# First weights and first rows of two stages loaded in the stage ahead, and a third place for turned chunks

## The chip, the cores and the metric

The kernel runs on one core of a Trainium2 chip. The metric is the device time of one execution in microseconds (us), as a median of several runs. The engines named here are TensorE (PE; PEld is its weight load), VectorE (DVE), ScalarE (ACT), GpSimd (POOL) and SyncE (SP), whose queue (SPq) issues most of the DMAs.

## The reference

A transformer block with conditioning, and behind it a rotation of each row within a 64-dimensional subspace. Four sequences of 1024 rows, 576 columns wide:

```python
ada = silu(c) @ W_ada + b_ada
shift_msa, scale_msa, gate_msa, shift_mlp, scale_mlp, gate_mlp = split(ada, 6)
h = modulate(layernorm(x), shift_msa, scale_msa)
x = x + gate_msa * attention(h, W_qkv, b_qkv, W_proj, b_proj)
h = modulate(layernorm(x), shift_mlp, scale_mlp)
x = x + gate_mlp * (gelu(h @ W_fc1 + b_fc1) @ W_fc2 + b_fc2)   # FF = 2304
U, _ = qr(P)                                                   # 576 x 64
R = expm(A(cond))                                              # 64 x 64 for each sequence
z = x @ U
out = x + (z @ R - z) @ U.T
```

## The kernel before, in words

The kernel is a sequence of stages with a barrier of all engines between them; each stage makes its own tiles and semaphores, and what passes from one to the next goes through DRAM. Products are made in float32 precision from two parts: a high part (rounded to float32r) and a low part (the difference), so that a float32 product is three passes. The last four stages are attention, `stage_proj`, `stage_mlp` and `stage_rotate`. The 4096 rows are taken in groups of 512 (`GT`), eight in all; in the feed-forward in groups of 256 (`GM`), sixteen in all.

**Projection (`stage_proj`).** For each of the eight groups TensorE spreads reciprocal sums, projects the attention's output, and turns the normalised rows into the operand of the feed-forward. ScalarE writes the operand's high parts to `ht`, GpSimd the low parts, and SyncE stores each of the five chunks to `h2_s` (line 1219). GpSimd adds the rows onto `x2_s` by an accumulating DMA (line 1252). SyncE's program is written out in order: loads of later groups, the five stores of this one, the wait for the accumulating DMA. Before its loop it loads the operand of the third group with lines 139 and 142.

**Feed-forward (`stage_mlp`).** All of `w1` (576 x 2304, two parts) and `w2` lie in SBUF, loaded in nine parts (`PARTS`) of two blocks (`PF`) of 128 hidden columns each. SyncE issues, in this order: `bias1` (line 1553), the first half group's operand `ht` (line 1544), then for each part four DMAs of `w1` (lines 65 and 67) and two of `w2` (line 1560), then the second `ht`, the gates and the `x` rows. TensorE runs two blocks ahead with `first` (14 matmuls, line 1655) and follows with `second` (12 matmuls, line 1669); between them ScalarE applies GELU (1593), VectorE makes the high part (1616), GpSimd the low part (1607). `first` waits for part `f // PF` of `w1` where a part begins, `second` for that of `w2`. At the end of a group VectorE adds and SyncE stores to `x3_s` (1571).

**Rotation (`stage_rotate`).** SyncE loads the rows of group 0 (line 1732), two parts of the rotated basis `ro` (1736), the basis `u` (1740), then the rows of group 1, and later those of group g + 2 within group g. GpSimd makes the identity matrix (146, 148) and pads the last 64 columns to 128 (1760). For each group TensorE turns five chunks of 512 x 128 (1817), each into one of two PSUM places, which chunk k takes as k % 2 (`c_slot`); ScalarE copies the high part (1769), VectorE subtracts for the low part (1787), and only then is the place free. Ten matmuls make z (1831), ScalarE and VectorE split it (1776, 1794), TensorE turns the next group's chunks, then makes y with 24 matmuls (1844), and VectorE adds the rows (1802). VectorE takes the next group's five low parts ahead of this group's eight sums; TensorE's 13th y matmul waits for the first sum.

## Time and profile before

| | |
|---|---|
| median of 3 runs | 3061.78 us (3058.14 to 3062.56) |
| the profiled execution | 3062.73 us |
| its span | 3061.1 us |
| TensorE busy | 2805.0 us, 92% |
| VectorE, ScalarE, GpSimd busy | 55%, 46%, 47% |
| feed-forward: SyncE's first issue, TensorE's first matmul | 1982.46, 1994.43 |
| rotation: SyncE's first issue, TensorE's first transpose | 2958.78, 2964.66 |

All times in rows are us from the span's start, durations of a single instruction ns where marked. The slices and the windows say what share of a stretch an engine was busy; the granted clock is TensorE's, as a share of its full 2.4 GHz, and the DMA share is the mean over 16 DMA engines. In a timeline an idle time stands in brackets, with what ended it. A busy TensorE isn't a TensorE at its peak, since the ends of matmuls are modelled.

### The profile page before, as it was taken

What the parts mean: (1) busy time and instruction counts of PE and PEld (TensorE: products, weight loads), DVE (VectorE), ACT (ScalarE), POOL (GpSimd) and SP (SyncE); (2) the same over time, 40 slices, a digit from 0 to 9 for tenths busy, and PEclk for the clock granted to TensorE, in tenths of its full rate; (3) what the DMA queues carried; (4) which work ended last, traced back from release to release, by engine and by line L of the source; (5) the groups of instructions that cost most, each with busy time, mean ns of one, the idle gap of its engine ahead of it and who ended that gap; (6) DMA issues with size and microseconds to landing.
All of it is one profiled execution on the core that took longest, in us unless ns stands there. A gap on an engine that the chain in (4) does not pass through costs nothing. (4 is left out here: it accounts for less than half of the span.)

```text
span 3061.1 us, 51443 instructions
## 1 busy us (share of the span) xinstructions
PE 2805.0 (92%) x16066; PEld 2272.3 (74%) x16066; DVE 1680.9 (55%) x3417; ACT 1416.8 (46%) x1835; POOL 1437.3 (47%) x1073
## 2 busy tenths in 40 slices
PE   7859999969999999999999879689999999999977
PEld 3248878846666666666666568589999999999976
DVE  4446777558999999999999657511111111111126
ACT  2112322229999999999999836511111111111112
POOL 1232333128888888888888836512222222222210
PEclk8769999979999999999999989899999999999989
DMA  5476675653443434343343259892112111211126
GB/s 191 136 245 228 228 249 196 234 170 85 89 93 83 95 81 94 85 90 91 85 96 81 71 165 289 246 310 74 37 38 66 46 38 37 74 38 37 53 74 217
DMA packets 336907, 377.68 MB, mean 123 GB/s; under 512 B 162816, under 2 KB 226952, under 8 KB 336764
## 3 DMA queue, kind: packets, MB, share of 16 engines
q1 hardware_dynamic: 327162, 356.66, 39.0%
q0 software_dynamic: 4224, 9.44, 1.7%
q10 hardware_dynamic: 5382, 9.67, 1.0%
q8 instruction: 95, 1.56, 0.2%
q14 instruction: 44, 0.36, 0.0%
HBM read 225.77 MB, written 158.93 MB: 126 GB/s over the span
## 5 line engine op out<-in xcount | busy, mean ns | idle before, releaser
L896 POOL TENSOR_TENSOR a_pl<-a_pf,a_ph 128x1024 fp32r<-128x1024 f32 x384 | 908.6, 2401 | 24.8 <-ACT a_pf L1006 24.8
L929 DVE TENSOR_REDUCE a_mx<-a_psum_s 128x1 f32<-128x512 f32 x992 | 637.5, 684 | 92.4 <-PE a_psum_s L1035 88.5
L1004 ACT ACTIVATE a_ph<-a_psum_t 128x1024 fp32r<-128x1024 f32 x512 | 525.9, 1027 | 133.6 <-PE a_psum_t L1052 126.5
L1607 POOL TENSOR_TENSOR m_al<-m_af,m_ah 128x256 fp32r<-128x256 f32 x288 | 211.1, 733 | 760.1 <-DVE m_ah L1616 760.1
L1655 PE MATMUL m_psum_h<-m_ht,m_w 128*128 128x256 f32 x4032 | 528.1, 283 | 30.2 <-DMA m_w<-w_s 20.5
L1616 DVE CAST m_ah<-m_af 128x256 fp32r<-128x256 f32 x288 | 85.1, 295 | 830.2 <-ACT m_af L1593 830.2
L1655 PEld LDWEIGHTS m_psum_h<-m_ht,m_w 128*128 128x128 f32 x4032 | 504.3, 189 | 33.7 <-issue 32.9
L1593 ACT ACTIVATE m_af<-m_psum_h,m_bias 128x256 f32<-128x256 f32 x288 | 136.4, 473 | 826.7 <-PE m_psum_h L1655 826.7
L1669 PE MATMUL m_psum_y<-m_w,m_ah 128*128 128x288 f32 x2304 | 506.7, 295 | 1.6 <-DVE m_y L1633 1.5
L1071 PE MATMUL a_psum_o<-a_ph,a_vs 128*100 128x512 f32 x1024 | 420.9, 411 | 22.4 <-POOL a_pl L896 18.9
L1072 PE MATMUL a_psum_o<-a_pl,a_vs 128*100 128x512 f32 x1024 | 405.1, 396 | 0.0
L1006 ACT ACTIVATE a_pf<-a_psum_t 128x1024 f32<-128x1024 f32 x384 | 391.2, 1019 | 0.0
L1669 PEld LDWEIGHTS m_psum_y<-m_w,m_ah 128*128 128x128 f32 x2304 | 388.1, 188 | 3.4 <-DVE m_y L1633 2.8
L1052 PE MATMUL a_psum_t<-a_qs,a_ks 110*128 110x512 f32 x1024 | 337.9, 412 | 37.8 <-DVE a_pl L945 31.3
L1669 PE MATMUL m_psum_y<-m_w,m_al 128*128 128x288 f32 x1152 | 341.3, 296 | 0.0
L1035 PE MATMUL a_psum_s<-a_ks,a_qs 108*128 108x512 f32 x992 | 313.9, 397 | 2.5 <-DVE a_mx L929 2.4
L1071 PEld LDWEIGHTS a_psum_o<-a_ph,a_vs 128*100 128x100 f32 x1024 | 168.7, 165 | 150.1 <-POOL a_pl L896 99.7
L1052 PEld LDWEIGHTS a_psum_t<-a_qs,a_ks 110*128 110x128 f32 x1024 | 184.5, 191 | 122.6 <-DVE a_pl L945 82.9
L663 PE MATMUL q_psum_pqk<-q_ht,q_w 128*128 128x512 f32 x1008 | 257.9, 408 | 13.3 <-DMA q_bv<-in_L_cond_b_qkv_dram 13.3
L1035 PEld LDWEIGHTS a_psum_s<-a_ks,a_qs 108*128 108x128 f32 x992 | 188.3, 190 | 64.9 <-DVE a_mx L929 3.6
L663 PEld LDWEIGHTS q_psum_pqk<-q_ht,q_w 128*128 128x128 f32 x1008 | 188.1, 192 | 55.6 <-issue 13.7
L1669 PEld LDWEIGHTS m_psum_y<-m_w,m_al 128*128 128x128 f32 x1152 | 216.6, 188 | 0.0
(232 smaller groups left out, 3059.5 us busy)
## 6 DMA issues: line engine op xcount, KB each, us to landing
a_qs<-q_s SPq DMA_DIRECT2D x192, 144.0 KB
a_ks<-k_s SPq DMA_DIRECT2D x192, 144.0 KB
w_s<-q_ws SPq DMA_DIRECT2D x64, 324.0 KB, 3.5
h_s<-p_ht SPq DMA_DIRECT2D x40, 512.0 KB, 4.7
m_ht<-h_s SPq DMA_DIRECT2D x16, 1280.0 KB, 8.2
v_s<-q_vo SPq DMA_DIRECT2D x64, 288.0 KB, 2.3
a_vs<-v_s SPq DMA_DIRECT2D x128, 144.0 KB, 4.5
q_s<-q_qko SPq DMA_DIRECT2D x32, 512.0 KB, 2.7
```

Of the source, the lines that this page charges most:

```text
L663: i = pe.matmul(pqk[:, m % 3], w[:, k, m * P:(m + 1) * P], ht[:, half, a, :], start=(n == 0), stop=(n == len(PASSES) - 1))
L896: pool.tensor_tensor(pl[:, s % RING], pf[:, s % RING], raw(ph[:, s % RING]), ALU.subtract).then_inc(lo_pool, 1)
L929: dve.tensor_reduce(mx[:, u % 2, t, h:h + 1], p_s[:, h * 512:(h + 1) * 512], AX.X, ALU.max) \
L1004: act.activation(ph[:, s % RING], p_t[:, s % 2], ACT.Exp, scale=SCALE)
L1006: act.activation(full, p_t[:, s % 2], ACT.Exp, scale=SCALE).then_inc(exp_done, 1)
L1035: pe.matmul(p_s[:, h * 512:(h + 1) * 512], qs[0:SROWS, u, t * P:(t + 1) * P], ks[0:SROWS, u, h * 512:(h + 1) * 512], start=True, stop=True) \
L1052: m = pe.matmul(p_t[:, s % 2, r * GT:(r + 1) * GT], ks[0:MROWS, u, t * P:(t + 1) * P], qs[0:MROWS, u, lh * GT:(lh + 1) * GT], start=True, ...
L1071: pe.matmul(p_o[0:VW, lh], vs[:, u, t], ph[:, s % RING, cols], start=(t == 0), stop=False)
L1072: m = pe.matmul(p_o[0:VW, lh], vs[:, u, t], pl[:, s % RING, cols], start=False, stop=(t == KT - 1))
L1607: pool.tensor_tensor(al[:, f % RING], af[:, f % RING], raw(ah[:, f % RING]), ALU.subtract).then_inc(lo_ready, 1)
L1655: m = pe.matmul(p_h[:, f % RING, 0:GM], w1[:, k, f * P:(f + 1) * P], ht[:, q, a], start=(i == 0), stop=(i == len(PASSES) - 1))
L1669: m = pe.matmul(p_y[:, t, a, 0:HALF], part[:, f % RING, t * P:(t + 1) * P], w2[:, s, f, a * HALF:(a + 1) * HALF], start=(f == 0 and i == 0 ...
```

## The change

Three things. (1) The feed-forward's weights part 0, its bias and the first half group's operand get tiles of their own, made before the projection on the right side of SBUF and kept until the end of the kernel (`mlp_tiles`). The projection loads them: the weights and the bias in seven DMAs ahead of SyncE's loop, the operand behind group `NG - 3`. SyncE waits for them at the end of the stage. The feed-forward starts with part 1. (2) When the last but one feed-forward group is stored, SyncE loads the basis `u`, and, once TensorE has done with part 0, the rows of the rotation's groups 0 and 1 into the homes of these weights. The rotation doesn't load them; the padding goes to a tile of its own, in two copies a group. (3) The rotation's turned chunks have three PSUM places instead of two (`SLOTS`).

```diff
@@ -54,6 +54,10 @@
+MLP_PARTS = 9
+MLP_PF = FF // P // MLP_PARTS
...
@@ -131,6 +135,23 @@
+def mlp_tiles(nc, ctx):
+    sb = lambda n, s, d=F32: ctx.enter_context(nc.sbuf_tensor("f_" + n, s, d, side="right"))
+    return {"w1": sb("w1", [P, W_TILES, MLP_PF * P], F32R),
+            "w2": sb("w2", [P, 2, MLP_PF, C], F32R),
+            "ht": sb("ht", [P, A_TILES, GT // 2], F32R),
+            "bias1": sb("bias1", [P, FF // P])}
+def load_mlp_weights(eng, w1, w2, w1_s, w2_s, i, w1_in, w2_in):
+    cols = slice(i * MLP_PF * P, (i + 1) * MLP_PF * P)
+    load_split_weight(eng, w1, w1_s, cols, w1_in)
+    for s in range(2):
+        eng.dma_start(raw(w2[:, s]), w2_s[s, cols].rearrange("(f p) n -> p f n", p=P)).then_inc(w2_in, 16)
...
@@ -1143,6 +1164,7 @@
+        first_w1, first_w2, first_h = sem("first_w1"), sem("first_w2"), sem("first_h")
...
@@ -1204,6 +1226,10 @@
+                load_mlp_weights(sp, first["w1"], first["w2"], w1_s, w2_s, 0, first_w1, first_w2)
+                sp.dma_start(first["bias1"][:], b1.rearrange("(f p) -> p f", p=P),
+                             allow_slow_non_contiguous=True).then_inc(first_h, 16)
...
@@ -1228,6 +1254,14 @@
+                    if g == NG - 3:
+                        for c in range(NK):
+                            sp.wait_ge(h_out[c], START + 16)
+                        sp.dma_start(raw(first["ht"][:]), h2_s[0:1, :, :, 0:GT // 2]
+                                     .rearrange("a p k n -> (a p) k n")).then_inc(first_h, 16)
+                sp.wait_ge(first_h, 32)
+                sp.wait_ge(first_w1, 64)
+                sp.wait_ge(first_w2, 32)
...
@@ -1498,18 +1532,20 @@
-    PARTS = 9
-    PF = FT // PARTS
+    PARTS, PF = MLP_PARTS, MLP_PF
-        w1 = sb("w1", [P, W_TILES, FF], F32R)
-        w2 = sb("w2", [P, 2, FT, C], F32R)
-        bias1 = sb("bias1", [P, FT])
+        w1 = sb("w1", [P, PARTS - 1, W_TILES, PF * P], F32R)
+        w2 = sb("w2", [P, PARTS - 1, 2, PF, C], F32R)
+        bias1 = first["bias1"]
-        ht = sb("ht", [P, 2, A_TILES, GM], F32R)
+        ht1 = sb("ht1", [P, A_TILES, GM], F32R)
+        ht = (first["ht"], ht1)
+        w1_part = [first["w1"]] + [w1[:, i] for i in range(PARTS - 1)]
+        w2_part = [first["w2"]] + [w2[:, i] for i in range(PARTS - 1)]
...
@@ -1518,7 +1554,7 @@
-        bias_in = sem("bias_in")
+        rows_in, u_in = sem("rows_in"), sem("u_in")
...
@@ -1541,7 +1577,7 @@
-                    sp.dma_start(raw(ht[:, q]), h2_s[bass.ds(j, 1), :, :, q * GM:(q + 1) * GM]
+                    sp.dma_start(raw(ht[q][:]), h2_s[bass.ds(j, 1), :, :, q * GM:(q + 1) * GM]
...
@@ -1550,15 +1586,8 @@
-                sp.dma_start(bias1[:], b1.rearrange("(f p) -> p f", p=P),
-                             allow_slow_non_contiguous=True).then_inc(bias_in, 16)
-                load_h(0, 0)
-                for i in range(PARTS):
-                    cols = slice(i * PF * P, (i + 1) * PF * P)
-                    load_split_weight(sp, w1[:, :, cols], w1_s, cols, w1_in[i])
-                    for s in range(2):
-                        sp.dma_start(raw(w2[:, s, i * PF:(i + 1) * PF]),
-                                     w2_s[s, cols].rearrange("(f p) n -> p f n", p=P)).then_inc(w2_in[i], 16)
+                for i in range(1, PARTS):
+                    load_mlp_weights(sp, w1_part[i], w2_part[i], w1_s, w2_s, i, w1_in[i], w2_in[i])
...
@@ -1575,15 +1604,28 @@
+                    if isinstance(n, int) and n == NG - 2:
+                        sp.dma_start(raw(ru[:]), u_s).then_inc(u_in, 16)
+                        for t in range(NT):
+                            sp.wait_ge(y_out[t], START + 16 * 4)
+                        sp.wait_ge(h_ready, FT * (NG - 1) + PF)
+                        sp.dma_start(raw(first["w1"][:]).rearrange("p k n -> p (k n)").rearrange("p (t c) -> p t c", c=C),
+                                     x3_s[0:GT].rearrange("(t p) c -> p t c", p=P)).then_inc(rows_in, 16)
+                        sp.wait_ge(used, RING + FT * (NG - 1) + PF)
+                        sp.dma_start(raw(first["w2"][:]).rearrange("p s f n -> p (s f n)")
+                                     .rearrange("p (t c) -> p t c", c=C),
+                                     x3_s[GT:2 * GT].rearrange("(t p) c -> p t c", p=P)).then_inc(rows_in, 16)
+                sp.wait_ge(u_in, 16)
+                sp.wait_ge(rows_in, 32)
-                act.wait_ge(bias_in, 16)
...
@@ -1645,21 +1687,24 @@
-                    if f == 0:
+                    if f == 0 and q == 1:
-                    if q == 0 and f % PF == 0:
+                    if f == 0 and q == 0 and not (isinstance(n, int) and n == 0):
+                        pe.wait_ge(ht_in[q], 16 * j)
+                    if q == 0 and f >= PF and f % PF == 0:
-                        m = pe.matmul(p_h[:, f % RING, 0:GM], w1[:, k, f * P:(f + 1) * P], ht[:, q, a],
+                        m = pe.matmul(p_h[:, f % RING, 0:GM], w1_part[f // PF][:, k, f % PF * P:(f % PF + 1) * P], ht[q][:, a],
-                    if q == 0 and f % PF == 0:
+                    if q == 0 and f >= PF and f % PF == 0:
...
@@ -1667,7 +1712,7 @@
-                                              w2[:, s, f, a * HALF:(a + 1) * HALF],
+                                              w2_part[f // PF][:, s, f % PF, a * HALF:(a + 1) * HALF],
...
@@ -1688,29 +1733,35 @@
-def stage_rotate(nc, x3_s, u_s, rot_s, out):
+def stage_rotate(nc, x3_s, rot_s, out, first, u):
+    EARLY = 2
+    SLOTS = 3
+    slot = lambda g, c: (NK * g + c) % SLOTS
-        u = sb("u", [P, NK, 2 * R], F32R)
-        xt = sb("xt", [P, NG, SUB, CPAD])
+        xt = sb("xt", [P, NG - EARLY, SUB, C])
+        pad = sb("pad", [P, NG, SUB, P])
+        rows = [raw(first["w1"][:]).rearrange("p k n -> p (k n)").rearrange("p (t c) -> p t c", c=C),
+                raw(first["w2"][:]).rearrange("p s f n -> p (s f n)").rearrange("p (t c) -> p t c", c=C)] \
+            + [xt[:, g] for g in range(NG - EARLY)]
-        p_t = ps("t", [P, 2, GT])
+        p_t = ps("t", [P, SLOTS, GT])
-        u_in, zeroed, ident_made = sem("u_in"), sem("zeroed"), sem("ident_made")
+        zeroed, ident_made = sem("zeroed"), sem("ident_made")
...
@@ -1729,16 +1780,16 @@
-                    sp.dma_start(xt[:, g, :, 0:C], x3_s[g * GT:(g + 1) * GT].rearrange("(t p) c -> p t c", p=P)) \
-                      .then_inc(x_in[g], 16)
+                    if g >= EARLY:
+                        sp.dma_start(rows[g], x3_s[g * GT:(g + 1) * GT].rearrange("(t p) c -> p t c", p=P)) \
+                          .then_inc(x_in[g], 16)
-                load(0)
-                sp.dma_start(raw(u[:]), u_s).then_inc(u_in, 16)
-                for g in range(1, AHEAD):
+                for g in range(AHEAD):
...
@@ -1755,9 +1806,13 @@
-                    pool.wait_ge(x_in[g], 16)
-                    pool.tensor_copy(xt[:, g, :, C:CPAD], xt[:, g, :, FULL * P:C]).then_inc(padded, 1)
+                    if g >= EARLY:
+                        pool.wait_ge(x_in[g], 16)
+                    for r in range(2):
+                        pool.tensor_copy(pad[:, g, :, r * REM:(r + 1) * REM], rows[g][:, :, FULL * P:C]) \
+                            .then_inc(padded, 1)
...
@@ -1766,7 +1821,7 @@
-                        act.activation(xh[:, half, c], p_t[:, c_slot(half, c)], ACT.Copy).then_inc(hi_ready, 1)
+                        act.activation(xh[:, half, c], p_t[:, slot(g, c)], ACT.Copy).then_inc(hi_ready, 1)
...
@@ -1799,7 +1854,7 @@
-                            dve.tensor_tensor(y[:, t, cols], p_y[:, t % 2, a, 0:HALF], xt[:, g, t, cols],
+                            dve.tensor_tensor(y[:, t, cols], p_y[:, t % 2, a, 0:HALF], rows[g][:, t, cols],
...
@@ -1807,20 +1862,20 @@
-                    pe.wait_ge(x_in[g], 16)
+                    if g >= EARLY:
+                        pe.wait_ge(x_in[g], 16)
-                            pe.wait_ge(padded, g + 1)
-                        if NK * g + c >= 2:
-                            pe.wait_ge(lo_ready, NK * g + c - 1)
+                            pe.wait_ge(padded, 2 * (g + 1))
+                        if NK * g + c >= SLOTS:
+                            pe.wait_ge(lo_ready, NK * g + c - SLOTS + 1)
-                            i = pe.transpose(p_t[:, c_slot(half, c), t * P:(t + 1) * P],
-                                             xt[:, g, t, c * P:(c + 1) * P], ident[:])
+                            i = pe.transpose(p_t[:, slot(g, c), t * P:(t + 1) * P],
+                                             rows[g][:, t, c * P:(c + 1) * P] if c < FULL else pad[:, g, t], ident[:])
-                pe.wait_ge(u_in, 16)
...
@@ -2318,12 +2373,15 @@
-    with ExitStack() as ctx:
-        early = proj_tiles(nc, ctx)
-        stage_attention(nc, q_s, k_s, v_s, o_t, sums, ada, gates2, x2_s, rsums, wproj_s, b_proj, early)
-        stage_proj(nc, o_t, sums, rsums, x_rows, ada, mod, x2_s, h2_s, early)
-    stage_mlp(nc, h2_s, x2_s, w1_s, b_fc1, w2_s, gates, x3_s)
-    stage_rotate(nc, x3_s, u_s, rot_s, out_rows)
+    with ExitStack() as late:
+        with ExitStack() as ctx:
+            early = proj_tiles(nc, ctx)
+            stage_attention(nc, q_s, k_s, v_s, o_t, sums, ada, gates2, x2_s, rsums, wproj_s, b_proj, early)
+            first = mlp_tiles(nc, late)
+            stage_proj(nc, o_t, sums, rsums, x_rows, ada, mod, x2_s, h2_s, early, first, w1_s, w2_s, b_fc1)
+        ru = late.enter_context(nc.sbuf_tensor("f_u", [P, FULL + 1, 2 * R], F32R, side="right"))
+        stage_mlp(nc, h2_s, x2_s, w1_s, w2_s, gates, x3_s, u_s, first, ru)
+        stage_rotate(nc, x3_s, rot_s, out_rows, first, ru)
```

The functions that it calls and that stand unchanged:

```python
def load_split_weight(eng, dst, src, cols, sem):
    for s in range(2):
        eng.dma_start(raw(dst[:, s * FULL:(s + 1) * FULL, :]),
                      src[s, 0:FULL * P, cols].rearrange("(k p) n -> p k n", p=P)).then_inc(sem, 16)
        eng.dma_start(raw(dst[s * REM:(s + 1) * REM, 2 * FULL, :]), src[s, FULL * P:C, cols]).then_inc(sem, 16)
```

## Rows read from the trace of the kernel before

**Rows 1.** The page, slices of 76.5 us: busy share of the DMA engines in tenths.

```profile
DMA  5476675653443434343343259892112111211126
```

**Rows 2.** Timeline of SyncE's queue: start, us, line, DMA, count.

```profile
1957.53 21.93 SPq L1219 DMA_DIRECT2D h_s<-p_ht  x10
1982.46 0.39 SPq L1553 DMA_DIRECT2D m_bias<-in_L_cond_b_fc_dram  x1
1982.90 1.52 SPq L1544 DMA_DIRECT2D m_ht<-h_s  x1
1984.47 0.78 SPq L65 DMA_DIRECT2D m_w<-w_s  x1
...
1986.49 1.37 SPq L67 DMA_DIRECT2D m_w<-w_s  x1
```

**Rows 3.** Timelines of TensorE and ScalarE, projection and first feed-forward group.

```profile
1804.46 6.08 PE L1455 MATMUL p_psum_p<-e_w,p_oh 128*128 128x288 f32 x28 [4.22 <-POOL p_oh L1242]
...
1811.77 3.98 PE L1455 MATMUL p_psum_p<-e_w,p_oh 128*128 128x288 f32 x28
...
1994.43 6.17 PE L1655 MATMUL m_psum_h<-m_ht,m_w 128*128 128x256 f32 x28 [18.78 <-DMA m_w<-w_s]
...
2050.81 1.93 PE L1655 MATMUL m_psum_h<-m_ht,m_w 128*128 128x256 f32 x14
...
2062.53 0.47 ACT L1593 ACTIVATE m_af<-m_psum_h,m_bias 128x256 f32<-128x256 f32 x1 [2.78 <-PE m_psum_h L1655]
```

**Rows 4.** Waits from 1982 to 2065: total us, times, longest.

```profile
PE m_psum_h L1655 <- DMA m_w<-w_s: 20.5, 3, 18.8
```

**Rows 5.** Chain that ended last, in the rotation: start, us, what.

```profile
2958.78 5.75 DMA r_xt<-x_s
...
2972.33 4.49 PE r_psum_z L1831 x10
```

**Rows 6.** Timeline of GpSimd at the rotation's start.

```profile
2959.14 0.29 POOL L148 TENSOR_SCALAR_AFFINE_SELECT r_ident<-r_ident 128x128 f32<-128x128 f32 x1 [0.15 <-POOL r_ident L146]
```

**Rows 7.** Windows: length, PE, PEld, DVE, ACT, POOL busy, granted clock, DMA share, GB/s.

```profile
1800.00:1810.00 10.00, 5.78 (x28) 5.55 (x27) 2.31 (x6) 2.75 (x4) 2.68 (x2) 0.66 0.65 201
1810.00:1820.00 10.00, 9.52 (x61) 7.92 (x60) 9.06 (x26) 6.19 (x12) 1.08 (x1) 1.00 0.87 198
1820.00:1830.00 10.00, 8.90 (x68) 8.12 (x66) 6.84 (x12) 6.98 (x11) 9.44 (x8) 1.00 0.40 129
1830.00:1840.00 10.00, 9.33 (x60) 7.82 (x58) 6.97 (x21) 5.74 (x12) 3.85 (x4) 1.00 1.09 334
...
2010.00:2020.00 10.00, 8.98 (x72) 8.75 (x71) 0.89 (x3) 1.42 (x3) 2.20 (x3) 1.00 1.09 339
...
2975.00:2977.00 2.00, 2.00 (x9) 1.59 (x8) 0.00 (x0) 0.16 (x1) 0.00 (x0) 0.62 0.22 46
...
2985.09:2995.80 10.71, 8.48 (x56) 7.16 (x55) 6.77 (x16) 3.37 (x6) 0.40 (x1) 1.00 0.65 222
```

**Rows 8.** Timelines of TensorE, VectorE and ScalarE in one rotation group.

```profile
2987.37 1.04 PE L1817 MATMUL r_psum_t<-r_ident,r_xt 128*128 128x128 f32 x8
2989.54 1.25 PE L1817 MATMUL r_psum_t<-r_ident,r_xt 128*128 128x128 f32 x8 [1.14 <-DVE r_xl L1787]
2991.70 0.63 PE L1817 MATMUL r_psum_t<-r_ident,r_xt 128*128 128x128 f32 x4 [0.90 <-DVE r_xl L1787]
...
2994.10 1.86 PE L1844 MATMUL r_psum_y<-r_ro,r_z 128*128 128x288 f32 x12 [0.19 <-DVE r_y L1802]
...
2988.81 1.28 DVE L1787 TENSOR_TENSOR r_xl<-r_psum_t,r_xh 128x512 fp32r<-128x512 f32 x2
...
2993.60 3.00 DVE L1802 TENSOR_TENSOR r_y<-r_psum_y,r_xt 128x288 f32<-128x288 f32 x8
...
2988.06 1.08 ACT L1769 ACTIVATE r_xh<-r_psum_t 128x512 fp32r<-128x512 f32 x2
```

**Rows 9.** Waits from 1800 to 1982, projection.

```profile
ACT p_rs L1390 <- DMA e_rs_f<-rsums: 0.2, 1, 0.2
```

**Rows 10.** Timeline of TensorE at the rotation's start.

```profile
2964.66 1.94 PE L1817 MATMUL r_psum_t<-r_ident,r_xt 128*128 128x128 f32 x8 [11.42 <-DMA r_xt<-x_s]
```

6 lines of the change are left out of this document (3 added, 3 removed).

## The prediction

> **What bounds the kernel now.** I read the page first. Its slices show the DMA engines at eight or nine tenths in four slices only, those of the projection and of the first feed-forward group, and at one or two tenths in the rest of the feed-forward [rows 1]. The change touches two stage boundaries, so I read these next. At the first, the feed-forward starts at 1982.46 with a load of the bias, then one of the operand `ht`, and the first of nine weight parts only at 1984.47 [rows 2]; TensorE has been idle for 18.78 us when its first matmul starts at 1994.43 [rows 3]. Nothing but the landing of these transfers holds it: of the 20.5 us that it waits for weights in this group, 18.8 are this one wait [rows 4]. At the second boundary the chain of waits begins with the rows' load, issued at 2958.78 and landed 5.75 us later [rows 5], while the identity matrix that the transposes also need is there at 2959.14 + 0.29 = 2959.43 [rows 6]. Behind it the rotation runs in groups of 10.71 us (2985.09 to 2995.80) [rows 7], in which TensorE waits 1.14 us for VectorE in the middle of the five turned chunks and 0.90 ahead of the fifth [rows 8]. All three stretches lie on the path: TensorE works in program order and the stage ends with its last group.
>
> **Feed-forward start.** The bias, `ht` for group 0 and part 0 of both weights leave the head of the stage. What is late next is part 1 of `w1`, wanted for the third block of 128 hidden columns. TensorE starts at about 1982.7 instead of 1994.43; its first 28 matmuls take 6.17 us at the lower clock [rows 3], so it wants part 1 at 1988.9. SyncE issues part 1 first. It is 1152 KB in four DMAs, whose fourth was issued 2.0 us behind the first (1984.47, 1986.49) [rows 2]; the nearest row is the rotation's load of the same size in one DMA, 5.75 us [rows 5]. With 0.75 us for the four issues I take 6.5 us, so it lands at 1989.0 (between 1988.2 and 1990.5). From there the stream of weights sets the pace, not TensorE: block 16, the first to need part 8, starts at 2050.81, so eight parts took 56.4 us, 7.05 each, with the DMA engines at a share of 1.09 and 339 GB/s [rows 3, 7], where TensorE needs only 2 x (2.78 + 0.47) = 6.50 us for a part [rows 3]. New start of block 16: 1989.0 + 7 x 7.05 = 2038.4, a gain of 12.4 us. If only TensorE's pace bound, it would be 1988.9 + 14 x 3.25 = 2034.4 or 16.4 us, which needs a faster stream than any shown. The second `ht` half, the gate and the `x` rows follow the stream in the same order and with the same distance to their users, so they move with it. ScalarE's wait for the bias goes, at no gain: TensorE's for the weights outlasts it.
>
> The Trainium skill (DMA: Bandwidth & Descriptors, section on the anatomy of one DMA) gives a fit of about 2.0 us plus bytes over 436 GB/s. An estimate by it is 2.0 + 2.7 = 4.7 us for these 1152 KB, and the gain would be 1.8 us larger; the trace has 5.75 us for that size, so the fit is not used [rows 5].
>
> **What the projection pays.** It takes in seven DMAs of 2.36 MB at its start (about 1804, behind the load of the third group's operand, ahead of that of the third group's `x`), and one of 1.31 MB near 1948. The seven cost SyncE some 4 to 6 us of issue. Queued behind them are the third group's `x` and gate rows, first used near 1836, and SyncE's next duty, a load that waits for VectorE until 1824.8 in any case: hidden. The engines' share is 0.65, 0.87 and 0.40 in the three stretches from 1800 on, against 1.09 when full [rows 7]; that leaves (0.44 + 0.22 + 0.69) x 10 = 13.5 us of room, of which perhaps 2 lie before 1804 and 3 after 1827, and 2.36 MB at 345 GB/s need 6.8. So it fits with little over. If it doesn't, the next in line is the small load of reciprocal sums, on which ScalarE already waits once, for 0.2 us [rows 9]: that load has no slack, and each us of backlog would go on the path. The second transfer is issued near 1948, ahead of SyncE's next issue at 1957.53 [rows 2], needs 1.31 MB / 345 GB/s = 3.8 us, and what is issued next is waited for only 12 us later. Bounds: 0 and 3.67 MB / 345 GB/s = 10.6 us; I take 0.3, since the room is there by the rows. The waits for these transfers at the stage's end are long satisfied. Net at this boundary: -12.1 us.
>
> A rule speaks against this change: by the Trainium skill (same page, section "Issuing engines are not separate DMA queues"), DMAs of all issuing engines run on the same 16 engines and interleave. The projection also has GpSimd's accumulating DMA in flight then, and is at 1.09 from 1830 to 1840 [rows 7]. Were no room left, moving bytes would buy nothing: 10.6 us come back, and the total would be near 3042.3. The stretches at 0.40 and 0.65 speak for the smaller price.
>
> **The last feed-forward group.** It gains three DMAs: the basis `u` and two sets of rows, 2.7 MB. SyncE's two new waits (the first operand blocks of the last group issued, the second block of the last group done) end within some 8 us of a group of 59, and behind them SyncE has nothing but the last stores, wanted at its end. The DMA engines are at one to two tenths there [rows 1]. Cost 0; if a wait lasted to the end, the price would be the load itself, the 5.75 us just removed.
>
> **Rotation start.** TensorE starts at 2959.5 instead of 2964.66 [rows 6, 10]: -5.2 us. GpSimd's padding is now two copies a group; the first pair is done 0.8 us after the identity, and the pad is needed 4 us after it. Later pairs run against groups that landed earlier. Cost 0, at most 0.4 us a group if one were late.
>
> **Third place, group 0.** At the lower clock eight transposes take 1.94 us [rows 10]. With two places the five chunks and their splits took 2964.66 to 2972.33, 7.7 us. With three, chunk 3 needs the low part of chunk 0, ready at about 1.1 + 0.6 + 0.7 = 2.5 us, while TensorE gets there at 2.9: no wait. Five chunks end at 5.0, ScalarE and VectorE finish the fifth at 6.4, so the z matmuls start at 6.5: -1.2 us.
>
> **Third place, seven times.** In the undisturbed group, counted from 2985.09 [rows 7, 8]: z matmuls to 2.28, chunks 0 and 1 after it, VectorE's low part of chunk 0 from 3.72, chunk 2 at 4.45, chunk 4 at 6.6, the sums of y from 8.51, TensorE's 13th y matmul at 9.01, next z at 10.71. With three places chunk 2 follows at 3.3 without a wait; ScalarE's copies are 0.48 apart, so VectorE does lows 0, 1, 2 from 3.72 in a row; chunk 3 starts at 4.45 (low 0 done) and chunk 4 at 5.06 (low 1 done); ScalarE copies chunk 4 at 5.7, VectorE's last low runs 6.4 to 7.0. The y matmuls start at 5.6, twelve are through at 7.2, the 13th waits for the first sum until 7.5, and 1.7 us later comes z, at 9.2. That is 1.5 us a group, seven times: -10.5 us. TensorE is busy for 8.5 us of the group and VectorE for 6.8 [rows 7], so neither bounds. The rows of group g+2 are issued about 1.3 us after z of g and wanted 11.5 us after it, against a landing of 5.75 us [rows 5].
>
> **Clock.** At the rotation's start TensorE is at the lower of its two levels (1.2 GHz); ten z matmuls take 4.49 us there [rows 5], against 2.3 in the undisturbed group, and the granted clock rises only in the stretch 2975 to 2977 (0.62) [rows 7]. There it worked with gaps before; the new five chunks run without one, as the 28 matmuls of the feed-forward did, which were through the lower level in 6.2 us. The rise may come before z: between 0 and 2.2 us, I take 0.8.
>
> **Sum.** -12.1 - 5.2 - 1.2 - 10.5 - 0.8 = -29.8 us. The profiled execution took 3062.7 (span 3061.1 and 1.6 around it), 0.9 over the median 3061.78. 3062.7 - 29.8 = 3032.9, for the median 3032.0.
>
> **Rivals.** (a) *The forecast*, within about 5 us: chance 0.62. (b) *The projection doesn't hide its transfers*: 3 to 10.6 us back, 3035 to 3042.3. For it: the share of 1.09 right behind the free stretch and the load without slack; against it: the room of 0.40 and 0.65. Chance 0.14. (c) *The third place frees little*, because another hand-over (ScalarE's order, the sums' semaphores) sets the group: at half its worth 3038, at none 3032.0 + 11.7 = 3043.7. Against it: both of TensorE's waits in the group are for VectorE's low parts. Chance 0.10. (d) *More than forecast*: the early clock and a faster stream, down to 3027 or a little below. Chance 0.07. (e) *The change doesn't do what it says*: part 1 lands some 10 us late because its stream starts slowly, or the rows' waits last to the stage's end; 12 + 5 us are lost, 3049. Chance 0.03. (f) *Slower than before*: the backlog in the projection makes TensorE wait in each of its six remaining groups, and it falls to the lower clock each time, as after the wait near 1804, where 28 matmuls took 6.08 us instead of 3.98 [rows 3]. With a wait w the price is 6 x (w + 2.1); it exceeds the 29.8 us from w = 2.9 us on, and at w = 4 the time is 3068.6. Against it: one backlog of 6.8 us, not one per group. Chance 0.04.
>
> **Chances and range.** This kernel's measurement tells apart about 0.2%, 6 us. (a) to (d) and the better part of (e) are faster by more: 0.95. Same 0.02 (a worse (e) and a weak form of (f)), slower 0.03. The range takes in the forecast, most of (d), and of (b) and (c) all but their ends: 3027 to 3041.
>
> **What would show it.** Right: first feed-forward matmul within 0.5 us of the stage's start, block 16 some 12.5 us sooner; the projection as long as before to 1 us; first transpose 0.1 us after the identity; the rotation's groups at 9.2 us, with no wait ahead of chunk 2 and one short wait ahead of chunk 3. Wrong: ScalarE or VectorE waiting for DMA in the projection; TensorE waiting more than 2 us for part 1; groups still over 10 us.

## The result, and the profile after

| | before | after |
|---|---|---|
| median of 4 runs | 3059.96 us (3054.84 to 3062.56) | 3023.27 us (3019.88 to 3028.35) |
| profiled execution, its span | 3062.73, 3061.1 us | 3026.63, 3025.0 us |

The changed kernel is faster: the ratio is 0.9884, with a 95% interval of 0.9861 to 0.9906. The medians differ by 36.7 us where 29.8 were forecast, and 3023.3 lies below the stated range of 3027 to 3041. That interval stands for a gain of 28.8 to 42.5 us, so the forecast gain lies just inside it and the forecast time outside its own range. Direction and main terms held; the size didn't.

Both spans are cut at SyncE's first DMA issue of a stage. Each length below is the difference of two such starts (the last one runs to the end of the span):

| stage | before | after | difference | forecast |
|---|---|---|---|---|
| all ahead of the projection | 1766.48 | 1761.13 | -5.4 | 0 |
| projection | 215.98 | 219.89 | +3.9 | +0.3 |
| feed-forward | 976.32 | 961.75 | -14.6 | -12.4 |
| rotation | 102.32 | 82.23 | -20.1 | -17.7 |

The slices of the page, as in [rows 1]; the busiest DMA slices are still those of the projection and the first feed-forward group:

```profile
PEclk9879999969999999999999979989999999999999
DMA  6386675653434343433343249992111211121127
```

The feed-forward's start, which answers to [rows 2] and [rows 3]. SyncE's queue (start us, length us, engine, line, operation):

```profile
1981.02 0.39 SPq L69 DMA_DIRECT2D m_w<-w_s  x1
```

And TensorE's timeline (idle time and what ended it in brackets):

```profile
1981.21 5.66 PE L1700 MATMUL m_psum_h<-f_ht,f_w 128*128 128x256 f32 x28 [7.03 <-PEq L1192]
1987.55 1.93 PE L1700 MATMUL m_psum_h<-f_ht,m_w 128*128 128x256 f32 x14 [0.68 <-DMA m_w<-w_s]
```

TensorE starts 0.2 us after the stage instead of 12.0. The next thing late is what the forecast named: part 1, landed 6.5 us after the stage's start. TensorE's waits in the first group, as in [rows 4]:

```profile
PE m_psum_h L1700 <- DMA m_w<-w_s: 2.8, 4, 0.8
```

18.8 us in one wait have become 2.8 in four. The projection takes in the seven added DMAs here; the last of them in SyncE's queue, with what follows:

```profile
1804.52 1.63 SPq L154 DMA_DIRECT2D f_w<-w_s  x2
1806.19 0.97 SPq L1231 DMA_DIRECT2D f_bias<-in_L_cond_b_fc_dram  x1
1807.56 12.70 SPq L1199 DMA_DIRECT2D p_xt<-in_x_dram  x1
```

Windows of the same stretch, as in [rows 7] (us, busy us of the five engines, granted clock, DMA share, GB/s):

```profile
1800.00:1810.00 10.00, 7.27 (x32) 6.96 (x32) 2.17 (x7) 2.74 (x4) 2.68 (x2) 0.66 0.85 231
1810.00:1820.00 10.00, 9.86 (x66) 8.51 (x64) 8.28 (x23) 6.96 (x13) 2.77 (x3) 1.00 1.08 258
1820.00:1830.00 10.00, 8.90 (x66) 8.27 (x66) 6.10 (x10) 7.66 (x11) 9.13 (x8) 1.00 0.93 310
```

The stretches that stood at 0.65, 0.87 and 0.40 are now at 0.85, 1.08 and 0.93: the room is used up. The next load's issue lasted 12.70 us, yet SyncE had nothing else due before 1823. The load without slack, [rows 9], waits 1.0 us in all now, 0.7 at the longest (ScalarE's wait of 4.8 us for an operand in the same stretch is there before and after):

```profile
ACT p_rs L1424 <- DMA e_rs_f<-rsums: 1.0, 2, 0.7
```

The rotation's start on TensorE, where [rows 5] and [rows 10] stood:

```profile
2943.48 3.68 PE L1873 MATMUL r_psum_t<-r_ident,f_w 128*128 128x128 f32 x16 [6.34 <-POOL r_ident L169]
2946.95 1.08 PE L1873 MATMUL r_psum_t<-r_ident,r_pad 128*128 128x128 f32 x4
2949.45 1.43 PE L1886 MATMUL r_psum_z<-r_xh,f_u 128*128 128x512 f32 x5 [1.41 <-DVE r_xl L1842]
```

Windows there, of TensorE alone (us, busy, granted clock, DMA share, GB/s):

```profile
2945.77:2947.77 2.00, 2.00 (x11) 0.50 0.97 200
2947.77:2949.77 2.00, 0.59 (x3) 0.82 0.95 343
2949.77:2951.77 2.00, 2.00 (x10) 1.00 1.08 273
```

One later group on TensorE, as in [rows 8]:

```profile
2958.81 1.32 PE L1886 MATMUL r_psum_z<-r_xh,f_u 128*128 128x512 f32 x5
2959.97 1.32 PE L1886 MATMUL r_psum_z<-r_xl,f_u 128*128 128x512 f32 x5
2961.13 1.48 PE L1873 MATMUL r_psum_t<-r_ident,r_xt 128*128 128x128 f32 x12
2963.31 0.66 PE L1873 MATMUL r_psum_t<-r_ident,r_xt 128*128 128x128 f32 x4 [0.70 <-DVE r_xl L1842]
2964.00 0.63 PE L1873 MATMUL r_psum_t<-r_ident,r_pad 128*128 128x128 f32 x4
2964.38 1.83 PE L1899 MATMUL r_psum_y<-r_ro,r_z 128*128 128x288 f32 x12
2966.40 1.86 PE L1899 MATMUL r_psum_y<-r_ro,r_z 128*128 128x288 f32 x12 [0.20 <-DVE r_y L1857]
2968.10 0.62 PE L1886 MATMUL r_psum_z<-r_xh,f_u 128*128 128x512 f32 x2
```

The group is the forecast one: three chunks in a row, one wait ahead of the fourth, 9.29 us. But at the start the clock has risen before z (0.82 on the mean of the window up to 2949.77, 1.00 in the next), so five z matmuls take 1.43 us where they took 2.47. That is more than the 0.8 us taken for it.

### The profile page after: what moved, and what is told of

It is laid out like the page before. It is cut to its first block and busy times, and to the rows that moved or that the text cites. A ratio compares the mean times of both kernels' runs of the same rounds, so it can differ in the third digit from the quotient of the medians.

```text
span 3025.0 us, 51433 instructions
## 1 busy us (share of the span) xinstructions
PE 2795.9 (92%) x16066; PEld 2270.6 (75%) x16066; DVE 1679.3 (56%) x3417; ACT 1416.8 (47%) x1835; POOL 1441.5 (48%) x1081
## 5 line engine op out<-in xcount | busy, mean ns | idle before, releaser
L1635 ACT ACTIVATE m_af<-m_psum_h,f_bias 128x256 f32<-128x256 f32 x288 | 136.8, 475 | 813.3 <-PE m_psum_h L1700 813.3
L1714 PE MATMUL m_psum_y<-m_w,m_ah 128*128 128x288 f32 x2048 | 448.1, 296 | 0.0
L1714 PEld LDWEIGHTS m_psum_y<-m_w,m_ah 128*128 128x128 f32 x2048 | 340.9, 188 | 0.0
L1714 PE MATMUL m_psum_y<-m_w,m_al 128*128 128x288 f32 x1024 | 299.2, 292 | 0.0
L1700 PE MATMUL m_psum_h<-f_ht,m_w 128*128 128x256 f32 x1792 | 235.8, 282 | 12.0 <-issue 9.1
L1700 PEld LDWEIGHTS m_psum_h<-f_ht,m_w 128*128 128x128 f32 x1792 | 224.5, 188 | 15.2 <-issue 14.3
L1700 PE MATMUL m_psum_h<-m_ht,m_w 128*128 128x256 f32 x1792 | 230.5, 279 | 0.0
```

The costliest lines, as they stand in the source:

```text
L1700: m = pe.matmul(p_h[:, f % RING, 0:GM], w1_part[f // PF][:, k, f % PF * P:(f % PF + 1) * P], ht[q][:, a], start=(i == 0), stop=(i == len(P ...
L1714: m = pe.matmul(p_y[:, t, a, 0:HALF], part[:, f % RING, t * P:(t + 1) * P], w2_part[f // PF][:, s, f % PF, a * HALF:(a + 1) * HALF], start ...
```

## Experiments

All kernels start from the changed one. "Pace" is the mean distance of ScalarE's activations of consecutive blocks in one feed-forward group, without the first three distances, which carry the change of groups and the way back of the loop; it is good to about 0.002 us. Odd and even groups (q = 1 and q = 0) keep their operand in different homes. Before, the pace was 3.253 us in both; after, it is 3.260 in even and 3.223 in odd groups. proj_burst, rows_late, two_warm and the six kernels that move homes ran once each, so they are read by the stages of their one trace.

### One part of the change at a time

**rot_only**: weights part 0, bias and operand loaded in the feed-forward, into the homes of the change.

```diff
-                load_mlp_weights(sp, first["w1"], first["w2"], w1_s, w2_s, 0, first_w1, first_w2)
-                sp.dma_start(first["bias1"][:], b1.rearrange("(f p) -> p f", p=P),
...
-                for i in range(1, PARTS):
+                sp.dma_start(bias1[:], b1.rearrange("(f p) -> p f", p=P),
+                             allow_slow_non_contiguous=True).then_inc(bias_in, 16)
+                load_h(0, 0)
+                for i in range(PARTS):
```

> The changed kernel with weights part 0, bias and first operand loaded in the feed-forward again, in the old order, into the new homes: only the rows' early loads and the third place are left. Theory A: feed-forward stage 973.7 us (pace as in the changed kernel, start as before), rotation 82.2 us with groups of 9.27 us and z matmuls of group 0 taking 2.6 us; total 20 + 2.6 = 22.7 us below the kernel before. Rival B (the rows' loads cost the last feed-forward group something): the stage longer than 973.7 by more than 1 us.

Feed-forward 973.4 us, rotation 82.1, periods 9.29, ratio 0.9928 (0.9910 to 0.9945), 22.0 us by it where 22.7 were expected. Theory A. The rows' loads cost the last feed-forward group nothing: 65.5 us with them, 65.4 without (layout_only, below).

**two_places** and **rows_late** are two corners of the rotation's part.

```diff
-    SLOTS = 3
+    SLOTS = 2
```

> The changed kernel with two places for turned chunks instead of three; rows and basis still come early. It separates the third place from the early rows. Theory A (third place worth 1.4 us a group, independent of the rest): groups of 10.7 us with waits for VectorE of about 1 us ahead of the third and fifth chunks, rotation 82.2 + 7 x 1.4 + 1.2 = 93.2 us, and group 0's z matmuls still fast (2.6 to 3.5 us), since TensorE started its transposes at once. Rival B (the gapless transposes are what brings the clock up before z): z matmuls of group 0 at 4.5 us, rotation 95.1 us. Rival C (the third place frees little by itself, the groups became shorter because the rows come early): groups of 9.3 us, rotation below 84 us.

```diff
-                        sp.dma_start(raw(ru[:]), u_s).then_inc(u_in, 16)
...
-                    if g >= EARLY:
-                        sp.dma_start(rows[g], x3_s[g * GT:(g + 1) * GT].rearrange("(t p) c -> p t c", p=P)) \
-                          .then_inc(x_in[g], 16)
+                    sp.dma_start(rows[g], x3_s[g * GT:(g + 1) * GT].rearrange("(t p) c -> p t c", p=P)) \
+                      .then_inc(x_in[g], 16)
...
+                sp.dma_start(raw(u[:]), u_s).then_inc(u_in, 16)
```

> The changed kernel with the rotation's rows and basis loaded in the rotation again, but three places kept: the fourth corner beside the two kernels with two places. Theory A (the third place is worth 15 us because, beside 1.46 us a group, it lets TensorE's clock rise sooner behind the rows, whenever they come, and keeps it up): rotation 82.2 + 5.2 = 87.4 us, the clock at the full level some 5 us after the first transpose, no group over 9.5 us. Rival B (the clock's share needs the early rows): the clock rises only behind the z matmuls, as with two places, rotation 89.5 us or more.

Lengths of the rotation in us:

| | two places | three places |
|---|---|---|
| rows loaded in the rotation | 102.3 (before) | 87.4 (rows_late) |
| rows loaded early | 97.4 (two_places) | 82.2 (after) |

The early rows are worth 4.9 and 5.2 us, the third place 14.9 and 15.2; they add up. rows_late is its theory A to the tenth (87.4), and its clock rises before z though the rows come late. My 93.2 us for two_places was wrong by 4.2, and rival B's 95.1 still by 2.3: the third place is worth more than its waits. two_places shows where. Its start on TensorE:

```profile
2938.49 1.97 PE L1873 MATMUL r_psum_t<-r_ident,f_w 128*128 128x128 f32 x8 [6.35 <-POOL r_ident L169]
2941.02 1.97 PE L1873 MATMUL r_psum_t<-r_ident,f_w 128*128 128x128 f32 x8 [0.56 <-DVE r_xl L1842]
2943.63 1.09 PE L1873 MATMUL r_psum_t<-r_ident,r_pad 128*128 128x128 f32 x4 [0.65 <-DVE r_xl L1842]
2946.13 2.50 PE L1886 MATMUL r_psum_z<-r_xh,f_u 128*128 128x512 f32 x5 [1.41 <-DVE r_xl L1842]
```

And windows late in its rotation (columns as above):

```profile
3007.00:3009.00 2.00, 1.09 (x10) 1.00 0.76 300
3009.00:3011.00 2.00, 2.00 (x11) 0.51 0.00 0
3011.00:3013.00 2.00, 2.00 (x12) 0.63 0.27 104
```

z starts 8.36 us after the stage's start instead of 6.68 (1.7 us); the first period is 12.95 us against 9.36, of which 1.46 is the usual difference of 10.75 and 9.29 (2.1 us more); and one late group takes 11.83 us since the clock falls in it (1.1 us). With 7 x 1.46 = 10.2 that makes 15.1. Of the 2.1 us a part is chance, as the section on the clock shows.

**mlp_only**: the edit of rows_late and two places; of the change only the projection's loads are left.

```diff
-    SLOTS = 3
+    SLOTS = 2
```

> The changed kernel with the rotation's rows and basis loaded in the rotation again and two places: only the projection's early loads (weights part 0, bias, operand) are left. Theory A: feed-forward stage 961.8 us as in the changed kernel (12.0 us of start and 2.6 of pace below the 976.3 of before), projection from the load of the third group's operand to its end within 0.5 us of 180.3, rotation 101.2 to 102.3 us; total 14.5 us below the kernel before. Rival B (the early loads cost the projection part of what they save): projection 3 us or more longer. Rival C (the stages' gains depend on each other): rotation away from 101.2 to 102.3.

Feed-forward 963.2 us, rotation 102.5. One even group of the feed-forward takes 62.2 us among those of about 60.4, since the granted clock falls to 0.50 in it (2696 to 2699); ht_mid, below, has such a group too. Ratio 0.9959 (0.9944 to 0.9974), 12.5 us: theory A within its interval. From the load of the third group's operand to the projection's end it took 180.6 us.

**layout_only**: the edits of rot_only and rows_late and two places; the placement of the tiles is left, and with it the padding in two copies, which costs nothing here (rotation as before).

```diff
-    SLOTS = 3
+    SLOTS = 2
```

> The changed kernel with its tiles where the change puts them, but every load back in the stage that uses it and two places for turned chunks: only the placement in SBUF is left of the change. Theory A (placement sets TensorE's pace in the feed-forward): blocks of 3.26 us in even groups and 3.22 us in odd ones, as in the changed kernel; the feed-forward stage, from SyncE's first issue to that of the rotation, takes 976.3 - 2.6 = 973.7 us, the first block wait is back (first matmul some 12 us after the stage's start), and the rotation takes 101.2 to 102.3 us. Total 2.6 us below the kernel before. Rival B (the pace came with the early loads or with the clock of that run): blocks of 3.25 us in all groups, 976.3 us, total as before.

Theory A. Feed-forward 973.1 us, rotation 102.3, pace 3.260 and 3.223; ratio to the kernel before 0.9987 (0.9974 to 0.9999), which is hardly clear of no change. The median, 3054.7, is 2.7 us under that of the kernel before in the same comparison (3057.3). The stage is the better witness: placement alone makes the feed-forward 3.2 us shorter (976.3 to 973.1), through TensorE's pace.

### The clock

**two_warm** and **warm**: 40 matmuls that nobody reads, behind the feed-forward's last, with two and with three places.

```diff
                 groups(nc.tensor, body)
+                for i in range(40):
+                    pe.matmul(p_h[:, 0, 0:GM], w1_part[1][:, 0, 0:P], ht1[:, 0], start=True, stop=True)
```

> The kernel with two places and early rows, with the 40 matmuls behind the feed-forward that keep TensorE busy until the stage's end. It takes the clock out of the comparison of two with three places. Theory A (of the 15.2 us between two and three places 10.2 are the groups' waits and the rest is mostly clock): granted clock 1.00 from the start, z 6.7 us after the stage's start instead of 8.36 with matmuls at half their length, rotation 97.4 - 1.7 - 2.6 = 93.1 us; one group of 11.8 us among those of 10.75 still there if the fall of the clock late in the rotation comes from its gaps, 92.0 us if not. Rival B (the difference is waits alone): 96 us or more.

> The changed kernel with 40 matmuls of one pass, whose result nobody reads, behind TensorE's last matmul of the feed-forward: some 4.7 us of work within the 5.5 us that the stage's last sums and stores take. It tests the clock's term at the rotation's start. Theory A (the rotation starts at the lower level because TensorE is idle for 6.3 us before it): the first five chunks run at 2.4 GHz, z starts 4.9 to 5.2 us after the stage's start instead of 6.68, its ten matmuls take 2.3 us instead of 2.6, rotation 80.2 us instead of 82.2; feed-forward unchanged. Rival B (the level falls with the stage's end whatever TensorE does, or the remaining idle time of 1.5 us is enough): 82.2 us. Rival C (the matmuls delay the stage's end): feed-forward longer by what they overlap.

two_warm on TensorE:

```profile
2944.03 1.10 PE L1875 MATMUL r_psum_t<-r_ident,f_w 128*128 128x128 f32 x8 [1.68 <-POOL r_ident L169]
2946.11 1.25 PE L1875 MATMUL r_psum_t<-r_ident,f_w 128*128 128x128 f32 x8 [0.98 <-DVE r_xl L1844]
2948.27 0.94 PE L1875 MATMUL r_psum_t<-r_ident,r_pad 128*128 128x128 f32 x4 [0.91 <-DVE r_xl L1844]
```

Its windows:

```profile
2945.32:2947.32 2.00, 1.22 (x8) 1.00 1.02 270
2947.32:2949.32 2.00, 0.98 (x5) 0.78 0.90 250
2949.32:2951.32 2.00, 0.70 (x2) 0.50 1.05 364
```

warm on TensorE:

```profile
2940.23 1.53 PE L1875 MATMUL r_psum_t<-r_ident,f_w 128*128 128x128 f32 x12 [1.68 <-POOL r_ident L169]
2942.30 0.66 PE L1875 MATMUL r_psum_t<-r_ident,f_w 128*128 128x128 f32 x4 [0.54 <-DVE r_xl L1844]
```

Its windows:

```profile
2941.51:2943.51 2.00, 1.43 (x11) 1.00 1.02 272
2943.51:2945.51 2.00, 0.59 (x3) 1.00 0.92 272
2945.51:2947.51 2.00, 2.00 (x11) 1.00 1.07 364
```

Both begin at the full level. With two places TensorE waits 0.98 and 0.91 us between its pairs of chunks, and the clock falls before z: the rotation took 96.3 us, not 93.1, and my claim that the clock would stay up was wrong. (96.3 is what rival B said, but not by waits alone: the first period is 12.90 us, as without the added matmuls.) With three places it waits once, 0.54 us, and the clock stays at 1.00: rotation 80.9 us (1.3 less than 82.2, where 2.0 were expected). So behind the same added matmuls the clock falls with two places and stays up with three, in one trace of each. The fall late in the rotation goes the same way: it is in all five kernels with two places (one group of 11.8 us each) and in none of the thirteen with three. It isn't a sure consequence of the waits: with two places every later group has them (1.14 and 0.90 us, [rows 8]), and the clock falls in one of the seven. The Trainium skill describes this kind of loss (TensorE: Matmul & The Clock Gate, "A second HAM failure mode: psum-queue depth-cycling"): small idle times between groups of matmuls that turn over PSUM buffers let the clock swing. This pair of traces agrees.

The rise at the start isn't a property of the change alone. With two places and no added matmuls it came 11.9 to 12.6 us behind the first transpose in all four kernels; with three, 3.2 to 5.1 us behind it in nine and 9.0 and 9.5 us in two. It came before z in the changed kernel and in eight others with three places and no added matmuls, but after z in order_new and ht_last, whose instructions up to z are the same (five z matmuls in 2.50 us, and a first period 1.4 and 1.7 us above the later ones). So at the start 1.4 to 1.7 of the 2.1 us hang on when the clock rises, which one and the same code doesn't settle. By warm's ratio, 0.9886 (0.9867 to 0.9905) beside 0.9884, the added matmuls' 1.3 us can't be told from nothing in whole runs.

### The price of bytes in the projection

**proj_burst**:

```diff
+                    if g < NG - 1:
+                        k = g - (NG - 4) + 1
+                        sp.wait_ge(first_w1, 64 * k)
+                        sp.wait_ge(first_w2, 32 * k)
+                        load_mlp_weights(sp, first["w1"], first["w2"], w1_s, w2_s, 0, first_w1, first_w2)
...
-                sp.wait_ge(first_w1, 64)
-                sp.wait_ge(first_w2, 32)
+                sp.wait_ge(first_w1, 64 * 4)
+                sp.wait_ge(first_w2, 32 * 4)
```

> The changed kernel, in which the projection loads weights part 0 three more times, behind its groups 4, 5 and 6: 2.36 MB more in each of three groups, six more DMAs each time, nothing else. It prices bytes in the projection. Theory A (there is room): from the load of the third group's operand to the stage's end it takes 180.5 us as in the changed kernel, within 1 us. Rival B (backlog goes on the path, as in the prediction's rivals): each set costs up to 2.36 MB / 345 GB/s = 6.8 us, the stage is 3 to 20 us longer and TensorE or ScalarE waits for DMA. Rival C (only SyncE's issue time counts): 0 to 4 us in all.

From the load of the third group's operand to the end it took 192.6 us: theory A holds for a part of the stage, rival B for the other. From the last load of an attention operand (SyncE's line 160, for group 7) to the first store of group 6 it took 42.05 us, as in the changed kernel. From there to the end it took 37.35 us instead of 24.96, 12.4 us more. Windows of these two stretches (us, busy us of ScalarE, granted clock, DMA share, GB/s), in the changed kernel and in proj_burst:

```profile
1914.01:1956.06 42.05, 28.70 (x47) 1.00 0.90 259
1956.06:1981.02 24.96, 10.49 (x16) 0.62 0.96 294
```

```profile
1906.29:1948.34 42.05, 28.66 (x47) 1.00 1.04 312
1948.34:1985.69 37.35, 10.49 (x16) 0.59 1.02 325
```

GB/s times length say where the three sets went. In the first stretch 312 x 42.05 - 259 x 42.05 = 2.2 MB more were moved: one set, at no cost in time, and the DMA engines are then full (1.04). In the second stretch 325 x 37.35 - 294 x 24.96 = 4.8 MB more were moved, two sets: the second set, issued from 1938.98, landed only from 1948.9 to 1955.9. So 4.8 MB cost 12.4 us, near the 13.9 us that rival B's 345 GB/s give. SyncE's queue there:

```profile
1957.52 0.66 SPq L69 DMA_DIRECT2D f_w<-w_s  x1
...
1968.99 1.10 SPq L154 DMA_DIRECT2D f_w<-w_s  x2
1970.14 5.33 SPq L1245 DMA_DIRECT2D h_s<-p_ht  x5
```

ScalarE's wait from 1955 on (us in total, times, longest), which the changed kernel doesn't have in its last stretch from 1950:

```profile
ACT p_ht L1468 <- DMA h_s<-p_ht: 9.6, 5, 3.7
```

The third set stands in the queue between the stores of groups 6 and 7. The stores of group 6 must leave `p_ht` before ScalarE may write it again, and those of group 7 end the stage: they landed at 1985.2, the third set at 1978.9. The bytes are free as long as the engines have room, and cost about their transfer once they are full and such stores stand among them. Whether the same backlog would be free behind other loads wasn't run.

### Where the pace comes from

Six kernels move the homes of tiles and nothing else. The diff is ht_moved's, which also makes the home of even groups' `ht` ahead of those of weights part 0, at the top of SBUF. The others move a line in the same way: ht_mid `ht1` ahead of `w2`, ht_last `ht1` behind `y`, ring_last `af`, `ah` and `al` behind `y`, gt_mid `gt` ahead of `w2`. ht_swapped is rot_only with `ht = (ht1, first["ht"])`.

```diff
+        ht1 = sb("ht1", [P, A_TILES, GM], F32R)
         w1 = sb("w1", [P, PARTS - 1, W_TILES, PF * P], F32R)
         w2 = sb("w2", [P, PARTS - 1, 2, PF, C], F32R)
...
-        ht1 = sb("ht1", [P, A_TILES, GM], F32R)
```

> The changed kernel with both operands of the feed-forward at other addresses: ht of odd groups at the bottom of the stage's tiles (16512 bytes per partition instead of 168608), ht of even groups at the top of SBUF (219104 instead of 200672), the weights shifted accordingly. Theory A (the operands' addresses set the pace of the 14 matmuls of a block): the pace of odd groups leaves 3.223 us, that of even groups leaves 3.260. Rival B (the pace goes with the code of odd and even groups, or with tiles other than the operands): still 3.223 and 3.260. All other stages as in the changed kernel.

> The changed kernel with the operand of odd groups between the two weights (90240 bytes per partition, instead of 168608 behind them); all else as in the changed kernel. Theory A (a place near the tiles that the other engines use is what makes it 3.223 us a block): another pace, 3.25 to 3.27 as at 16512 bytes. Rival B (only the lowest and the highest addresses are slow): 3.223 stays. Even groups 3.260 in both.

> The changed kernel with the operand of odd groups behind all other tiles of the feed-forward, at 187040 bytes per partition (168608 in the changed kernel; in the kernel before one half of the operand began at 187136), and af, ah, al, xt, y 10240 bytes lower. Theory A (the operand's own address sets the pace): 3.253 us a block in odd groups, as before at that address. Theory B (the neighbourhood of af, ah and al does): another pace than 3.253, 3.26 as for the even groups, whose operand also lies apart from them. Even groups 3.260 in both.

> The changed kernel with af, ah and al behind xt and y (188064 to 197280 bytes per partition instead of 178848 to 188064), the operand of odd groups where it is (168608). Theory A (the operand's own address sets the pace): 3.223 us a block in odd groups stays. Theory B (the neighbourhood of af, ah and al does): 3.25 to 3.27. Even groups 3.260 under A, perhaps another under B, since the three tiles come nearer to their operand.

> The changed kernel with the gate's tile between the two weights: w2 begins at 94848 bytes per partition instead of 90240, everything else keeps its address. Theory C (the place of w2 sets the odd groups' pace): the 3.223 us a block of odd groups become 3.25 to 3.27, as in the two kernels with w2 at 100480. Theory D (it is a matter of the range in which the operand lies, fast at 168608 to 197280 and slow below 100480): 3.223 stays. Even groups 3.260 under D.

> The kernel with weights part 0, bias and operand loaded in the feed-forward, with the two homes of the operand exchanged: even groups use the tile at 168608, odd groups the one at 200672. Theory D (the home decides): even groups 3.223 us a block, odd ones 3.260. Theory E (the code of the group decides: even groups carry the waits for the weights): even groups 3.260 and odd ones 3.223 as before. Stage lengths as in the kernel with those loads and the homes not exchanged (973.4 us of feed-forward, 82.1 of rotation).

At how many bytes per partition things begin, and the pace in us a block:

| kernel | `ht` odd, even | `w2` | pace odd, even |
|---|---|---|---|
| after | 168608, 200672 | 90240 | 3.223, 3.260 |
| ht_moved | 16512, 219104 | 100480 | 3.265, 3.260 |
| ht_mid | 90240, 200672 | 100480 | 3.265, 3.260 |
| ht_last | 187040, 200672 | 90240 | 3.223, 3.260 |
| ring_last | 168608, 200672 | 90240 | 3.223, 3.260 |
| gt_mid | 168608, 200672 | 94848 | 3.223, 3.260 |
| ht_swapped | 200672, 168608 | 90240 | 3.260, 3.223 |

ht_swapped is the clearest: the fast pace moves with the home, not with the code. Neither the neighbouring tiles (ring_last, ht_last) nor `w2` at 94848 (gt_mid) matter. ht_last missed both of its theories, 3.253 and 3.26. ht_moved is rival B's for the even groups, whose pace stayed at the new address, and theory A's for the odd ones. ht_mid gave its theory A's number, but ring_last speaks against the reason that this theory gave. So the range in which the operand lies seems to decide: fast at 168608 and 187040, slow at 16512, 90240, 200672 and 219104. For the two lowest `w2` lay at 100480 as well, and no kernel parts the two. The difference lies in the 14 matmuls that read it; in the changed kernel they are 1.64 us start to start from the odd home and 1.67 from the even one:

```profile
2218.25 1.80 PE L1700 MATMUL m_psum_h<-m_ht,m_w 128*128 128x256 f32 x14
2219.89 0.29 PE L1714 MATMUL m_psum_y<-m_w,m_ah 128*128 128x288 f32 x1
...
2221.47 1.83 PE L1700 MATMUL m_psum_h<-f_ht,f_w 128*128 128x256 f32 x14
2223.14 0.30 PE L1714 MATMUL m_psum_y<-m_w,m_ah 128*128 128x288 f32 x1
```

In the kernel before the two halves began at 187136, next to an address that is fast here, and at 197376, and the pace was 3.253 for both; its `w1` had another layout. What draws the bounds of the range, and what part the layout has, stays open.

### Going further

**order_new**: the rotation in another order.

```diff
-                        transposes(g + 1, 1 - half)
+                        transposes(g + 1, 1 - half, range(3))
...
                     for t in range(SUB):
+                        if t == 2 and not last:
+                            transposes(g + 1, 1 - half, range(3, NK))
```

(VectorE's `lows` likewise.)

> The changed kernel with another order in the rotation: TensorE turns chunks 0 to 2 of the next group, does the y matmuls of row tiles 0 and 1, turns chunks 3 and 4, and does the y matmuls of tiles 2 and 3; VectorE does lows 0 to 2, the sums of tiles 0 and 1, lows 3 and 4, the sums of tiles 2 and 3. Theory A (what is left of the group's waits is TensorE's 0.7 us for the first low part and 0.2 for the first sum; both get cover): period 8.5 us instead of 9.29, set by VectorE's last low part; rotation 82.2 - 7 x 0.79 = 76.7 us. Rival B (the sums that now stand ahead of lows 3 and 4 hold z back): period 9.3 us or more.

Periods of 8.42 us, rotation 77.6; 76.7 were expected, and the late rise of the clock (1.4 us in the first period) makes the difference. Ratio 0.9859 (0.9843 to 0.9876).

**combined** adds to that order the 40 matmuls and a longer loop body in the feed-forward, since TensorE loses time on each way back:

```diff
-            with eng.Fori(0, NG // 2 - 1) as j:
-                body(2 * j, j, 0, False)
-                body(2 * j + 1, j, 1, False)
+            with eng.Fori(0, NG // 4 - 1) as i:
+                for k in range(4):
+                    body(4 * i + k, 2 * i + k // 2, k % 2, False)
...
+            for n in range(NG - 4, NG):
+                body(n, n // 2, n % 2, n == NG - 1)
```

> The changed kernel with three additions: the new order in the rotation, the 40 matmuls behind the feed-forward, and the feed-forward's loop with four groups in its body instead of two (three rounds of four and four groups written out, instead of seven rounds of two and two written out). Expected by stages: each way back of the loop costs TensorE 1.5 us (six of them in the changed kernel, two here), so the feed-forward takes 961.5 - 4 x 1.5 = 955.5 us; rotation 77.6 - 1.2 (start at the full level) - 2.2 (z at the full level) = 74.2 us; total 14 us below the changed kernel, about 3009 us. Rival B (the longer body has its own cost of fetching instructions): feed-forward 961 us or more. Rival C (the new order loses its gain once the clock is up): rotation 76 us or more.

TensorE's waits from 2100 to 2800, in the changed kernel and in this one:

```profile
PE m_psum_h L1700 <- issue: 9.1, 6, 1.7
```

```profile
PE m_psum_h L1700 <- issue: 3.0, 2, 1.7
```

Feed-forward 955.8 us, as expected. Rotation 76.1, against 74.2, which is rival C's number but not its reason: the periods are all 8.42, z starts 1.2 us sooner, but the first period gave back 1.4, not 2.2, and the last store landed 1.0 us later than in order_new. Median of five runs 3011.46 us (3007.34 to 3016.17), ratio 0.9849 (0.9831 to 0.9867): faster than the kernel before by 46 us. Beside the changed kernel it is some 11 us as the two ratios stand (by its stages 12), though their intervals just touch; and whole runs don't tell it from order_new.

## Why the prediction was right in kind and wrong in size

- **Feed-forward start**: right. -12.0 us to the first activation of group 1 (76.82 to 64.83 from the stage's start), -12.4 forecast. Block 16 starts 56.3 us after the stage's start instead of 68.4, 12.1 sooner. Part 1 landed at 6.5 us as said, and waits for the stream of weights remain.
- **Projection**: right in its term, 0.3. From the third group's operand load to the end it took 180.25 us before and 180.53 after. Over all profiles it is 180.0 to 180.6 in the four kernels without the early loads (mean 180.2) and 180.2 to 180.8 in the thirteen that carry them once (mean 180.5). The other 3.6 us stand ahead of the first added DMA (35.73 us before, 39.36 after) and go with a lower granted clock there (0.78 and 0.70 on the mean). proj_burst shows that the argument by free share was sound: one more set fitted into the room, and rival (b)'s price came when the engines were full.
- **A term that was missing, -2.6 us**: the rest of the feed-forward. The prediction took the pace as fixed (3.25 us a block) and gave no reason; a change of homes was worth nothing in its sum. layout_only shows that the new homes alone bring it.
- **Rotation start**: right: -4.9 and -5.2 in the two comparisons, -5.2 forecast.
- **Third place**: the failed step is its term for the clock. 12.5 us forecast (10.5 + 1.2 + 0.8), 15.2 measured. The waits were sized well (7 x 1.46 = 10.2, and 1.7 up to z). The clock was not: 0.8 was taken within 0 to 2.2, and it is 2.1 at the start and 1.1 late. The prediction worked with the "undisturbed group" seven times over; the kernel before had one group of 11.85 us, with the granted clock at 0.58 and 0.57 in 3024 to 3028, and every kernel with two places has one such. The start's share came out at the upper end of its bounds, and there luck has a part: in order_new and ht_last, with the same code up to z, 1.4 and 1.7 us of it didn't come. Rival (c) fell; the waits were the limit.
- **Stages ahead**: their code is unchanged, and the projection started between 1750.5 and 1766.5 us in the eighteen profiles, the latest of them in the kernel before. So the -5.4 there can't be put down to the change. The +3.6 in the projection's lead is less clear: it took 35.73 us in the one profile of the kernel before and 38.0 to 39.5 in all seventeen others, with early loads or without. They share the new placement, and no run tells that from chance.

In sum: -29.8 - 2.6 (placement) - 2.7 (third place) - 5.4 + 3.6 (lead) = -36.9, against -36.1 between the two spans; the rest is in the smaller terms above. Neither failed term alone leaves the range (3032.0 - 2.7 = 3029.3 and 3032.0 - 2.6 = 3029.4); both give 3026.7. The other 3.4 us down to 3023.3 are of the size of the stages ahead and the lead, for which no run shows a cause. Rival (d), "more than forecast, by the clock", was the case, at a chance of 0.07, and even its mechanism named only half of it. Rival (f) didn't occur: from 1800 us on no wait of TensorE for DMA came up in the projection. ScalarE's did, one of the signs of being wrong, but it is the 1.0 us above and moved nothing that shows.
